# First attention of a four-layer network: six stack and three output buffers, rows ahead of stacks, the split of maxima ahead of normalising

## The reference, cut to what matters

```python
for s in SHIFTS:                                   # (0, 2)
    for idx, (nh, hs, nw, ws) in enumerate(strip_params):   # two halves of the channels
        qkv = jnp.einsum('bchw,oc->bohw', xsp, wq)
        ...
        attn = jax.nn.softmax(jnp.einsum('whqc,whkc->whqk', qw, kw), axis=-1)
        ow = jnp.einsum('whqk,whkc->whqc', attn, vw) + lw
x = x + _L0_conv_ref(_gn(x), ...)
```

## Time and profile before

| | us |
|---|---|
| median of 3 runs | 4029.73 (4028.17 to 4032.12) |
| span of the profiled execution, first to last instruction | 4026.0 |
| first attention's loop, first exp to last copy | 335.06 to 787.63 |
| PE busy, whole span | 3440.5 (85%) |
| DVE busy, whole span | 2489.7 (62%) |
| ACT busy, whole span | 1927.2 (48%) |
| SP's DMAs (queue 1), share of 16 rings, whole span | 21.8% |

### The profile page before, as it was taken

The page is one execution under the profiler, slowest core; times in us unless marked ns, Lnnn a source line. Parts: engine busy times, 40 slices in busy tenths (PEclk is TensorE's granted clock), DMA queues, the critical chain, the costliest instruction groups (busy, mean ns, idle before and its releaser), DMA issues. The chain is left out here.

```text
span 4026.0 us, 66483 instructions
## 1 busy us (share of the span) xinstructions
PE 3440.5 (85%) x24463; PEld 1530.3 (38%) x24463; DVE 2489.7 (62%) x4082; ACT 1927.2 (48%) x2321; POOL 860.5 (21%) x866
## 2 busy tenths in 40 slices
PE   6997887647599999999999998789878479999999
PEld 4664555424322222222222221633567334444444
DVE  3227767465489999998999995344486323333333
ACT  1214667512147777777777777334323223233322
POOL 0001333300000000000000000034200245555555
PEclk9997778778779999999999999789989589999999
DMA  4444555400500000000000000044101122222221
GB/s 144 125 126 103 115 118 119 88 1 2 180 18 16 21 21 21 22 20 21 15 26 21 16 21 6 17 138 150 53 0 43 33 81 85 84 87 85 84 84 47
DMA packets 137544, 247.17 MB, mean 61 GB/s; under 512 B 34808, under 2 KB 47264, under 8 KB 136800
## 3 DMA queue, kind: packets, MB, share of 16 engines
q1 hardware_dynamic: 137312, 243.98, 21.8%
HBM read 171.55 MB, written 56.62 MB: 57 GB/s over the span
## 5 line engine op out<-in xcount | busy, mean ns | idle before, releaser
L1073 DVE TENSOR_REDUCE mxv<-mx_ps 128x1 f32<-128x512 f32 x2048 | 1276.9, 683 | 88.8 <-PE mx_ps L932 70.6
L1048 ACT ACTIVATE PT<-st_ps 128x1024 f32<-128x1024 f32 x1024 | 997.1, 1022 | 297.3 <-PE st_ps L945 297.1
L932 PE MATMUL mx_ps<-KS,QS 24*128 24x512 f16 x2048 | 613.3, 394 | 114.0 <-DVE mxv L1073 96.6
L1921 DVE TENSOR_TENSOR u<-h_ps,s 128x512 f32<-128x512 f32 x352 | 243.5, 692 | 541.6 <-ACT s L1899 494.6
L959 PE MATMUL o_ps<-PT,VA 128*32 128x512 f32 x4096 | 550.0, 609 | 0.5 <-ACT PT L1048 0.5
L1951 POOL TENSOR_TENSOR hg<-u,gb 128x512 f32<-128x512 f32 x352 | 450.9, 1283 | 394.1 <-DVE u L1921 297.4
L1899 ACT ACTIVATE s<-h_ps 128x512 f32<-128x512 f32 x352 | 210.2, 597 | 587.3 <-PE h_ps L1875 587.3
L1883 PE MATMUL y_ps<-hg,m_w 128*128 128x512 f32 x704 | 361.4, 597 | 55.2 <-POOL hg L1951 55.1
L945 PE MATMUL st_ps<-QS,KS 26*128 26x512 f16 x2048 | 400.4, 387 | 9.2 <-ACT TX L1038 8.5
L667 DVE TENSOR_REDUCE mxv<-mx_ps 128x4 f32<-128x512 f32 x512 | 319.7, 683 | 118.3 <-PE mx_ps L542 113.8
L945 PEld LDWEIGHTS st_ps<-QS,KS 26*128 26x128 f16 x2048 | 96.5, 91 | 558.2 <-issue 479.7
(11 more groups left out here) (228 smaller groups left out, 4173.1 us busy)
## 6 DMA issues: line engine op xcount, KB each, us to landing
gb<-g SPq DMA_DIRECT2D x64, 512.0 KB, 3.7
gb<-g SPq DMA_DIRECT2D x16, 2048.0 KB
QK<-qk SPq DMA_DIRECT2D x128, 192.0 KB
qk<-hl SPq DMA_DIRECT2D x80, 256.0 KB, 3.3
RB<-d SPq DMA_DIRECT2D x48, 256.0 KB, 3.5
qk<-hl SPq DMA_DIRECT2D x64, 128.0 KB, 3.2
v<-vs SPq DMA_DIRECT2D x32, 256.0 KB
VS<-v SPq DMA_DIRECT2D x32, 256.0 KB, 3.1
```

The costliest lines, as they stand in the source:

```text
L932: nc.tensor.matmul(mx_ps[:, use % 3, :], rows(QS, g // 2, j, STACK)[:, t * C:(t + 1) * C], rows(KS, g // 2, j, STACK)[:, half * HALF:(half ...
L1048: nc.scalar.activation(PT[:, n % 2, 2 * a:2 * a + 2], st_ps[:, a], ACT.Exp, scale=1.0 / SHIFT ** 2).then_inc(st_free[a], 1)
L1073: nc.vector.tensor_reduce(mxv[:, g % 2, j, t, half:half + 1], mx_ps[:, slot], AX.X, ALU.max).then_inc(mx_free, 1)
```

## The change

It gives the stage six stack buffers and three output buffers, numbered by a running group number `4 * i + u`; loads a stack five groups ahead rather than three; reorders SP's list, so that DEN and the rows come first and the stack behind them; cuts `spread` in two, so that the reciprocals are stored one group ahead of being read back; and lets POOL split before it normalises, half 0 in group 3 of its own image and half 1 in group 1 of the next. DVE inverts two steps earlier. The fill of ones becomes six memsets of float32 words, each holding two float16 ones, with a count for each. The waits on `regrouped` and `den_loaded` get a semaphore a unit.

```diff
+MAX_UNITS = 2.0 ** 113 * (1 + 30720 / 2.0 ** 23)
...
+    STACKS, OUTS = 6, 3
...
+    def group(i, u):
+        return i * U + u
+    def stack(i, u):
+        return group(i, u) % STACKS
...
-        QK = chip.buf(ctx, "QK", [C, U, 2, S, N], F16)
+        QK = chip.buf(ctx, "QK", [C, STACKS, 2, S, N], F16)
-        OR = chip.buf(ctx, "OR", [C, 2, S, N])
+        OR = chip.buf(ctx, "OR", [C, OUTS, S, N])
...
-                def spread(i, h):
+                def store_inverse(i, h):
                     count = i * 2 + (h + 2)
                     sp.wait_ge(x_done, count)
                     sp.wait_ge(inverted, count)
                     sp.dma_start(d_scr[i, h].rearrange("a p n -> p a n"), RD[:]).then_inc(rd_stored, 16)
+                def spread(i, h):
                     sp.wait_ge(rd_stored, i * 32 + (16 * h + 32))
                     for part in range(2):
...
-                sp.wait_ge(ones_set, 1)
-                load_qk(0, 0)
-                load_v(0, 0)
-                load_qk(0, 1)
-                load_v(0, 1)
-                load_qk(0, 2)
-                load_qk(0, 3)
+                for g in range(5):
+                    sp.wait_ge(ones_set, g + 1)
+                    load_qk(g // U, g % U)
+                    if g < 2:
+                        load_v(0, g)
...
                         if i or u:
                             sp.wait_ge(st_ready[1], i * STEPS + 4 * u)
-                        if u == 0 and kind != "first":
-                            load_qk(i, 3)
-                        if u and kind != "last":
-                            load_qk(i + 1, u - 1)
+                        if group(i, u):
+                            load_den(i - (u == 0), (u + 3) % U)
                         if kind != "last" or u < 3:
                             sp.wait_ge(mx_free, i * PER + (LEAD + MX[kind]["turn", u, TURNS[u][-1]] + 1 + 3))
-                            load_rows((u + 1) % 4)
-                        if u:
-                            load_den(i, u - 1)
-                            regroup(i, u - 1)
-                        elif kind != "first":
-                            load_den(i - 1, 3)
-                            regroup(i - 1, 3)
-                        if kind != "last" or u < 1:
-                            sp.wait_ge(va_done, i * U + (u + 2))
-                            load_v(i + (u + 3) // 4, (u + 3) % 4)
+                            load_rows(i + (u == 3), (u + 1) % U)
                         if u == 3:
                             spread(i, 0)
                         if u == 1 and kind != "first":
                             spread(i - 1, 1)
+                        if group(i, u) + 5 < B * U:
+                            load_qk(i + (u + 5) // U, (u + 5) % U)
+                        if group(i, u):
+                            regroup(i - (u == 0), (u + 3) % U)
+                        if kind != "last" or u < 1:
+                            sp.wait_ge(va_done, i * U + (u + 2))
+                            load_v(i + (u + 3) // 4, (u + 3) % 4)
+                        if u == 2:
+                            store_inverse(i, 0)
+                        if u == 0 and kind != "first":
+                            store_inverse(i - 1, 1)
...
-                    if n % 4 == 0:
-                        act.wait_ge(regrouped[u % 2], i * 256 + (u // 2 * 128 + 128))
-                        act.wait_ge(den_loaded[u % 2], i * 32 + (u // 2 * 16 + 16))
+                    g = group(i, u)
+                    if n % 4 == 0 and g >= OUTS:
+                        before = g - OUTS
+                        act.wait_ge(regrouped[before % U], 128 * (before // U + 1))
+                        act.wait_ge(den_loaded[before % U], 16 * (before // U + 1))
...
-                nc.vector.memset(KS, MAX_UNIT).then_inc(ones_set, 1)
+                for k in range(STACKS):
+                    nc.vector.memset(KS[:, k].rearrange("p s n -> p (s n)").bitcast(F32), MAX_UNITS).then_inc(ones_set, 1)
...
-                        if n == 5 and kind != "first":
+                        if n == 3 and kind != "first":
                             invert(i - 1, 1)
-                        if n == 13:
+                        if n == 11:
                             invert(i, 0)
...
-                        if u % 2 == 0 and kind != "first":
-                            finish(i - 1, u // 2)
                         if kind != "last" or u < 2:
                             split_max(u, i * PER + (LEAD + MX[kind][4 * u + 3, 1] + 1 + 3), i * 12 + (3 * u + 6))
+                        if u == 1 and kind != "first":
+                            finish(i - 1, 1)
+                        if u == 3:
+                            finish(i, 0)
...
-                finish(LAST, 0)
                 finish(LAST, 1)
```

More of the change, by code:

```diff
@@ L433, in window_attention @@
         o_ps = chip.psum(ctx, "o_ps", [C, HALF])
-        qk_loaded = [chip.sem("qk_loaded") for _ in range(U)]
-        rows_loaded, v_loaded, den_loaded, rb_loaded, regrouped, st_ready, st_free = ([chip.sem(s) for _ in range(2)] for s in (
-            "rows_loaded", "v_loaded", "den_loaded", "rb_loaded", "regrouped", "st_ready", "st_free"))
+        qk_loaded = [chip.sem("qk_loaded") for _ in range(STACKS)]
+        den_loaded, regrouped = ([chip.sem(s) for _ in range(U)] for s in ("den_loaded", "regrouped"))
+        rows_loaded, v_loaded, rb_loaded, st_ready, st_free = ([chip.sem(s) for _ in range(2)] for s in (
+            "rows_loaded", "v_loaded", "rb_loaded", "st_ready", "st_free"))
         (filled, ones_set, mx_ready, mx_free, split, va_done, pv_done, o_free, inverted, rd_stored,
@@ L451, in load_qk, with load_rows @@
                 def load_qk(i, u):
+                    k = stack(i, u)
                     for j in range(4):
[L453 to L454 removed]
+                        sp.dma_start(QK[32 * j:32 * j + STACK, k].rearrange("p o s n -> p o (s n)"),
+                                     qk_scr[i, u, :, :, j].rearrange("o r s n -> r o (s n)")).then_inc(qk_loaded[k], 16)
                 def load_v(i, u):
                     sp.dma_start(VS[:, u % 2], v_scr[i, u]).then_inc(v_loaded[u % 2], 16)
[L459 removed]
+                def load_rows(i, u):
                     for c in range(2):
[L461 removed]
+                        sp.dma_start(QS[STACK + c:C:32, stack(i, u)].rearrange("j s n -> j (s n)"),
                                      mT[64 * c:64 * c + 64, u % 2]).then_inc(rows_loaded[u % 2], 16)
@@ L466, in load_den @@
                     sp.wait_ge(o_free, i * STEPS + (4 * u + 5))
-                    sp.dma_start(DEN[:, u // 2, u % 2], OR[D:C:32, u % 2].rearrange("j s n -> j (s n)")).then_inc(den_loaded[u % 2], 16)
+                    o = group(i, u) % OUTS
+                    sp.dma_start(DEN[:, u // 2, u % 2], OR[D:C:32, o].rearrange("j s n -> j (s n)")).then_inc(den_loaded[u], 16)
                 def regroup(i, u):
@@ L530, in _ @@
                 regroup(LAST, 3)
+                store_inverse(LAST, 1)
                 spread(LAST, 1)
@@ L534, in _, with rows, max_scores @@
             def _(pe):
-                def rows(buf, u, s, j, count):
-                    return buf[32 * j:32 * j + count, u, s]
-                def max_scores(u, n, j, use):
+                def rows(buf, k, s, j, count):
+                    return buf[32 * j:32 * j + count, k, s]
+                def max_scores(k, n, j, use):
                     for w in range(4):
@@ L542, in max_scores @@
                         mm = nc.tensor.matmul(mx_ps[:, use % 3, w * C:(w + 1) * C],
-                                              rows(QS, u, n // 2 % 2, j, STACK)[:, at],
-                                              rows(KS, u, n // 2 % 2, j, STACK)[:, at], start=True, stop=True)
+                                              rows(QS, k, n // 2 % 2, j, STACK)[:, at],
+                                              rows(KS, k, n // 2 % 2, j, STACK)[:, at], start=True, stop=True)
                     mm.then_inc(mx_ready, 1)
@@ L549, in turn, with scores @@
                                         ident[:]).then_inc(mx_ready, 1)
-                def scores(n, a):
-                    u, s = n // 4, n // 2 % 2
+                def scores(i, n, a):
+                    k, s = stack(i, n // 4), n // 2 % 2
                     if a == 1:
-                        fill_array(nc, st_ps[:, a, 1], ident, KS[:, u, s, 0:HALF])
+                        fill_array(nc, st_ps[:, a, 1], ident, KS[:, k, s, 0:HALF])
                     for w in range(4):
@@ L557, in scores @@
                         for e in range(2):
-                            mm = nc.tensor.matmul(st_ps[:, a, e, w * C:(w + 1) * C], rows(KS, u, s, 2 * a + e, ROWS)[:, at],
-                                                  rows(QS, u, s, 2 * a + e, ROWS)[:, at], start=True, stop=True)
+                            mm = nc.tensor.matmul(st_ps[:, a, e, w * C:(w + 1) * C], rows(KS, k, s, 2 * a + e, ROWS)[:, at],
```

(12 more changed lines are left out.)

14 lines of the change are left out of this document (7 added, 7 removed).

## The result

The change takes 3998.84 us (median of 4 runs, 3983.52 to 4003.26) beside 4030.93 for the kernel before: a ratio of 0.9916, 95% interval 0.9896 to 0.9935. Run once more, in the first set of experiments, it took 3986.13 (3974.06 to 3995.94), 0.9898 (0.9874 to 0.9922). The forecast was 3980.8, with 3932 to 4008 as its range. Beside the 4029.73 that it started from, that is a gain of 48.9 us; 32.1 were measured, and 43.9 in the rerun. The profiled execution is the fastest of its four: its own time is 3983.52, its span 3981.7, against 4026.0.

A forecast was written before the change was run, and what follows sets the result against it. Late rows of negated maxima, stuck behind spread and stack on SP's DMA queue, and the slowed clock lose 87.6 us. Span 4026.0 - 42.6 - 3 - 3.3 = 3977.1; median lies 3.7 higher: 3980.8 us, range 3932 to 4008.

The forecast's parts named there:

- Part 1: SP's list in the attention loop: rows issued ahead of spread and stack; 42.6 of 87.6 us lost come back.
- Behind a group with a spread they are still late: Next group's rows of negated maxima (`QK<-mT`) land at 11.7, needed at 10.3: late by 1.4 us.
- over two groups the rings need 25.1: DMA rings, a spread plus two groups' stack, rows, regroup, v, DEN; taken as 26.0 against VectorE's 22.28 us.
- the high end: Upper bound on the rings' time for two groups: today's pair, 388.04 / 14 = 27.7 us.
- Rival (a): Attention loop: rows always in time, pair cost 22.3 or less, all 87.6 us come back, 3936 us; chance 15%.
- Rival (c): SP stands 7.5 us at the spread for the stored reciprocals, delaying the next rows; slower, 4085 us; chance 6%.
- Parts 2 and 3: SP's own issue time, and extra buffers, GpSimd's split before normalising and moved reciprocals: all costed at nothing.
- Two more stacks let SP load five groups ahead: Part of the buffers and orders in the attention loop that were said to cost nothing; no gain booked.
- Parts 4 and 5: Attention's start, fill as six memsets: -3 us (bounds -1 and -4.5); its end, last normalising earlier: -3.3 us.

The follow-up runs named there:

- the light spread: The change with the spread's loads bringing 8 partitions in place of 64, an eighth of the bytes, rest of `RB` ones: 3935.2 us, ratio 0.9759.

## Why the prediction was right, and where it was not

**Part 1, the size.** The forecast took 42.6 us back in the loop; the profiled run has 29.1, the rerun 38.1 (388.04 - 349.9). The start gave 4.2 where 3 were booked, the end 3.6 where 3.3 were, and 6.7 came in stages behind, which nobody had booked. So the sum, 3977.1 us of span against 3981.7, is closer than its largest term, and that is luck: 13.5 us too much in the loop are half made up by 6.7 in other stages, in an execution that is 15.3 us faster than the median. The median lies 18.0 above the forecast.

**Part 1, what is late.** "Behind a group with a spread they are still late" was right of the backlog, and wrong of what it holds up. Waits for rows were to be 15 to 25 us and are 5.5; 19.0 us of waits for instructions, which the forecast did not have, make 24.5 together. Behind both the clock falls: behind the longest wait it is granted at its lower level, 0.50, from 416.0 to 436.0 us. The stretch was to take about 345 us at a clock near 0.9: 358.9 at 0.85, and 349.9 at 0.89 in the rerun.

**Part 1, "over two groups the rings need 25.1", taken as 26.0.** This is the step that failed. Landing times of one order were added up and read as a need. The same bytes go through in 314.2 / 13.5 = 23.3 us a pair with the stack first, and 0.5 MB more in 23.9. The 26.0 was a property of the order, in which a spread ahead of a stack makes the packets slower. It came near the change's 358.9 / 13.5 = 26.6 because the change keeps that order. There is a slip beside it: the stretch has 27 groups and not 28, so a pair took 28.7 us before, and that, not 27.7, is the high end; 300.4 is the sum for 27.

**Rival (a)** was given 15% and 3936 us as the price of a loop without late rows. The change doesn't reach it. The version with four stacks, stack first, does by its time (3937.7), though its loop keeps 13.8 us of loss (314.2 against 300.4). A stack there lands 4.6 to 6.9 us after SP has issued it, with a median of 5.6; in the change the median is 9.1. The rule of the Trainium skill by which a stack runs on 12 engines and a spread on 8 (DMA: Bandwidth & Descriptors, the section on why a DMA increments its semaphore by 16) agrees with the stretches: a spread by itself and spread and stack together in the change have shares of 0.50 and 0.75, 8 and 12 of 16.

```profile
573.00:574.50 1.50, 1.50 (x49) 0.98 (x41) 1.40 (x4) 1.35 (x3) 0.00 (x0) 1.00 0.50 153
576.00:579.50 3.50, 3.28 (x101) 2.10 (x89) 3.29 (x6) 3.13 (x5) 2.19 (x4) 1.00 0.75 172
```

The larger share brought little here: 172 GB/s for 153.

**Rival (c)**, SP standing at the spread for the store, hardly occurs in the change (5.5 us in 5 stands, of up to 2.4). It does with the store put back, at 1.8 us a stand rather than 7.5: the mechanism exists, and the earlier store is what keeps it small.

**Parts 2 and 3.** GpSimd's order is worth nothing, as booked. The third output is not free of effect: without it TensorE waits 33.4 us for the copy. "Two more stacks let SP load five groups ahead" was costed at nothing without asking what four would do: they would make this order slower than the kernel before.

**Parts 4 and 5.** The memsets take 0.91 us each (0.87 forecast). SP's first load goes out 4.0 us earlier, where 6 were forecast, and the first maxima move only from 314.33 to 312.83. Most of what is missing is the stage before, which ends 3.5 us later in this execution: counted from there the first maxima come 5.0 us earlier, where some 4 were forecast, and in the six experiments with the same start they begin at 309.3 to 310.8, near the forecast's 310 (the rerun, where that instruction begins at 299.26, has 312.41). VectorE's credits come last there: its memset of `VA` ends at 312.61. The end is as booked.

## What to carry to other kernels

Where transfers share one list, look for the order before buying buffers: here the stack first, spread behind the rows, gave 2.3% with the memory of four stacks, and the change's order gave 0.9% with six. Don't read a chain of landing times as what the rings need; move the pieces, or add a load, and see whether the chain's length is a capacity. And when a wait shrinks less than its cause should let it, look in the rows without a releaser: what is late may be the engine's own instructions, or a wait that the profile can't name, and the time since the last instruction packet tells which.

## What the runs showed of the hardware that was not expected

- TensorE can stand for its own instructions. Each such wait ends 1.3 to 1.9 us behind a 16 KB packet on queue 8, one of which comes for 254 matmuls and weight loads; they come to 19.0 us in the change, 2.1 with stack and spread swapped, and 0.3 with the light spread. That the packet is late because of the data beside it follows from these three runs; its path was not seen.
- Packets of the same transfers took 203 us with the spread ahead of the stack, 180 with the stack ahead, 181 where SP waits for the spread.
- SP can stand 75.8 us in this loop without changing the time (3989.1 against 3986.1), where what it holds back travels faster (181 us of packets for 203).
